# Product of du and B for both channel halves in one 1024-wide VectorE instruction, with the states in a ring of three pairs

## What is computed

```
def step(state, xs):                       # 256 steps along the tokens
    d_t, B_t, C_t, u_t = xs
    dA = jnp.exp(d_t[..., None] * A)
    state = state * dA + (d_t * u_t)[..., None] * B_t[:, None, :]
    y_t = jnp.einsum('ben,bn->be', state, C_t)
    return (state, y_t)
...
x = x + tanh(g_xattn) * ssm(ctx, layernorm(x))       # y = (scan + D*u) * silu(z)
x = x + tanh(g_ffn) * routed_moe(layernorm(x))       # 8 experts, top 2, hidden width 512
```

## Time and profile before

| | |
|---|---|
| median of 3 runs | 307.88 us (307.65 to 309.58) |
| time of the profiled execution | 307.61 us |
| its span | 305.8 us |
| PE busy | 265.8 us (87%) |
| DVE (VectorE) busy | 229.0 us (75%) |
| ACT (ScalarE) busy | 188.4 us (62%) |
| POOL (GpSimd) busy | 183.2 us (60%) |
| mean granted TensorE clock | 0.959 of full |

### The profile page before, as it was taken

One profiled execution on the slowest core, in us unless ns is written; L12 is line 12 of the kernel. 1 busy time (PEld: TensorE's weight loads), 2 busy tenths in 40 slices (PEclk: granted clock), 3 DMA queues, 4 the chain that ended last, 5 costly groups with the idle time before them and its releaser, 6 DMA issues.

```text
span 305.8 us, 4685 instructions
## 1 busy us (share of the span) xinstructions
PE 265.8 (87%) x1166; PEld 178.1 (58%) x1167; DVE 229.0 (75%) x398; ACT 188.4 (62%) x349; POOL 183.2 (60%) x162
## 2 busy tenths in 40 slices
PE   8984698789788999897889489999999999999970
PEld 8432243234234345363565357988889898888960
DVE  2839999997889999999899664656565665656640
ACT  1894577865765685768484844565665657566540
POOL 5000449996999898998590442355547465565442
PEclk9996979999999999999999778999999999999996
DMA  7699200000000000001059611123242332423222
GB/s 233 225 395 387 94 2 0 0 1 0 0 0 3 1 0 0 0 2 69 1 184 331 242 49 39 29 41 57 48 69 40 63 51 52 68 35 69 28 26 34
DMA packets 16659, 22.70 MB, mean 74 GB/s; under 512 B 2554, under 2 KB 10274, under 8 KB 16642
## 3 DMA queue, kind: packets, MB, share of 16 engines
q1 hardware_dynamic: 11456, 16.41, 15.2%
q0 software_dynamic: 4416, 6.03, 11.9%
q10 hardware_dynamic: 770, 0.06, 0.2%
HBM read 17.38 MB, written 5.11 MB: 74 GB/s over the span
## 4 chain that ended last, share of the span: by engine, by line
PE 54%; DVE 23%; issue 11%; ACT 6%; POOL 3%; POOLq 1%; DVEq 0%; ACTq 0%
PE PD L1025 11%; PE PZ L1061 11%; PE PU L1025 10%; PE PY L844 7%; DVE states L1216 6%; DVE states L1222 5%; PE PY L1047 3%; DVE u L1142 2%; POOL hC L411 2%; PE PZ L1016 2%; PE PU L823 1%; PE PU L830 1%; PE PU L752 1%; ACT PD L612 1%; DVE WO L1240 1%
## 5 line engine op out<-in xcount | busy, mean ns | idle before, releaser
L411 POOL TENSOR_TENSOR hC<-states,WO 128x512 f32<-128x512 f32 x63 | 79.5, 1272 | 19.6 <-DVE states L1222 9.2
L1222 DVE TENSOR_TENSOR_SCAN states<-PD,states 128x512 f32<-128x512 f32 x64 | 77.3, 1209 | 1.3 <-ACT PD L612 1.0
L844 PE MATMUL PY<-hC,ident 128*128 128x512 f32 x128 | 68.9, 623 | 7.2 <-POOL hC L411 6.9
L446 POOL DMA_INDIRECT out<-lg,y_at x23 | 36.4, 1581 | 49.3 <-ACT lg L718 41.9
L612 ACT ACTIVATE PD<-WO,Aneg 128x510 f32<-128x510 f32 x64 | 43.9, 688 | 18.2 <-DVE states L1222 15.5
L1216 DVE TENSOR_TENSOR states<-PU,WO 128x512 f32<-128x512 f32 x64 | 42.7, 668 | 2.7 <-POOL hC L411 1.6
L402 POOL TENSOR_TENSOR W_lo<-W,W_hi 128x512 fp32r<-128x512 f32 x25 | 32.5, 1308 | 11.5 <-ACT W_hi L523 11.5
L1459 DVE TENSOR_TENSOR dA<-PU,dA 128x512 f32<-128x512 f32 x23 | 15.9, 691 | 28.5 <-PE PU L1025 28.5
L702 ACT ACTIVATE hidT_hi<-PY 128x512 fp32r<-128x512 f32 x23 | 13.8, 598 | 38.0 <-PE PY L1047 38.0
L1471 DVE TENSOR_TENSOR WO_lo<-WO,WO_hi 128x512 fp32r<-128x512 f32 x46 | 29.7, 688 | 9.4 <-issue 9.3
L844 PEld LDWEIGHTS PY<-hC,ident 128*128 128x128 f32 x128 | 21.9, 191 | 23.4 <-POOL hC L411 17.3
(11 more groups left out here) (245 smaller groups left out, 507.2 us busy)
## 6 DMA issues: line engine op xcount, KB each, us to landing
W<-in_L_ffn_w SPq DMA_DIRECT2D x16, 512.0 KB, 10.9
WO<-in_L_ffn_wo SPq DMA_DIRECT2D x8, 512.0 KB, 8.4
xs<-in_x SPq DMA_DIRECT2D x2, 512.0 KB, 5.5
out<-xs SPq DMA_DIRECT2D x2, 512.0 KB, 3.2
x_rows<-u SPq DMA_DIRECT2D x2, 512.0 KB, 5.9
early<-in_ctx SPq DMA_DIRECT2D x1, 512.0 KB, 4.2
hC<-x_rows,x_at POOLq DMA_INDIRECT x23
out<-lg,y_at POOLq DMA_INDIRECT x23, 3.8
```

Of the source, the lines that this page charges most:

```text
L411: pool.tensor_tensor(hC[:, n % 2, :], states[:, n % RING, :], C_rep[:, pair % C_RING, :], ALU.mult).then_inc(hc_done, 1)
L446: pool.indirect_dma_start(out=out, out_offset=bass.IndirectOffsetOnAxis(ap=y_at[:, s:s + 1], axis=0), in_=y_tile[s % 2], in_offset=None, c ...
L844: pe.matmul(PY[:, h, :], ident[:, :], hC[:, n % 2, :], start=False, stop=(m == DS - 1)).then_inc(y_done, 1)
L1222: dve.tensor_tensor_scan(states[:, n % RING, :], DEC[n % 2], states[:, n % RING, :], 0.0, ALU.mult, ALU.add).then_inc(scan_done, 1)
```

## The change

The products of the two halves of a pair become one VectorE instruction of 128 x 1024: B is read twice through a stride of zero, du of both halves stands side by side already. Pair 0 keeps two narrow products (`first_drive`), since du of its second half comes later; the first counts up a semaphore of its own, `half_driven`. The slots are now in pairs: RING = 3 pairs, two of them in `states` (which stays at 4 slots, 2 * (RING - 1)), the third in `dA`. Pair p lies in slot (p + 1) % 3, slot 0 is `dA`, first used by pair 2, whose product therefore also waits for two logarithms (`sp_ln_ok`) and two roundings (`rest_ok`). The product of pair p waits for the hC product of state 2p - 5. `dbu_done` now counts pairs: 32 in all for 64, and its waits are halved.

```
-RING = 4
+RING = 3
...
-        states = sb("states", [P, RING, QT])
+        states = sb("states", [P, 2 * (RING - 1), QT])
...
+        def state_pair(pair):
+            slot = (pair + 1) % RING
+            return states[:, 2 * slot - 2:2 * slot, :] if slot else dA[:, :, :]
+        def state(n):
+            return state_pair(n // 2)[:, n % 2, :]
...
                 if pair:
-                    pe.wait_ge(dbu_done, 2 * pair)
+                    pe.wait_ge(dbu_done, pair)
...
-            def drive(n):
-                q, pair, h = n // (2 * DS), n // 2, n % 2
+            def first_drive(h):
+                dve.wait_ge(b_ps, 1)
+                dve.wait_ge(du_ok, h + 1)
+                dve.tensor_tensor(state(h), BCR[0], du[h], ALU.mult).then_inc(dbu_done if h else half_driven, 1)
+            def drive(pair):
+                q = pair // DS
                 dve.wait_ge(b_ps, pair + 1)
-                dve.wait_ge(du_pool if q else du_ok, h + 1)
-                if n >= RING:
-                    dve.wait_ge(hc_done, n - RING + 1)
-                dve.tensor_tensor(states[:, n % RING, :], BCR[pair % 2], du[2 * q + h], ALU.mult).then_inc(dbu_done, 1)
+                dve.wait_ge(du_pool if q else du_ok, 2)
+                if pair == RING - 1:
+                    dve.wait_ge(sp_ln_ok, 2)
+                    dve.wait_ge(rest_ok, 2)
+                if pair >= RING:
+                    dve.wait_ge(hc_done, 2 * (pair - RING + 1))
+                dve.tensor_tensor(state_pair(pair), BCR[pair % 2].rearrange("p (o t) -> p o t", o=1).to_broadcast((P, 2, QT)),
+                                  du_sb[:, q, :, :], ALU.mult).then_inc(dbu_done, 1)
...
             def through(at, end):
                 for n in range(at, end):
-                    if n + 1 < NT:
-                        drive(n + 1)
+                    if n % 2 and n + 1 < NT:
+                        drive(n // 2 + 1)
                     scan(n)
...
-            drive(0)
+            first_drive(0)
             scan(0)
             delta_sum(1)
             drive_input(1)
-            drive(1)
+            first_drive(1)
```

More of the change, by code:

```diff
@@ L257, in build @@
         diag_ok, gz_ok, x2_ps, logits_ok = sem("diag_ok"), sem("gz_ok"), sem("x2_ps"), sem("logits_ok")
+        half_driven = sem("half_driven")
         exp_done, dbu_done, scan_done, hc_done, y_done = map(sem, ("exp_done", "dbu_done", "scan_done", "hc_done", "y_done"))
@@ L337, in _ @@
             sp.wait_ge(exp_done, NT)
-            sp.wait_ge(dbu_done, NT)
+            sp.wait_ge(dbu_done, NT // 2)
             load_WO(0)
@@ L410, in times_C @@
                         pool.wait_ge(y_done, n - 1)
-                    pool.tensor_tensor(hC[:, n % 2, :], states[:, n % RING, :], C_rep[:, pair % C_RING, :], ALU.mult).then_inc(hc_done, 1)
+                    pool.tensor_tensor(hC[:, n % 2, :], state(n), C_rep[:, pair % C_RING, :], ALU.mult).then_inc(hc_done, 1)
                     if n in SPLIT_AT:
@@ L984, in _ @@
                 add_gz(1, r)
-            pe.wait_ge(dbu_done, NT)
+            pe.wait_ge(dbu_done, NT // 2)
             pe.wait_ge(c_ok, NT // 2)
@@ L1207, in _ @@
             rounding(1)
-            def drive(n):
-                q, pair, h = n // (2 * DS), n // 2, n % 2
-                dve.wait_ge(b_ps, pair + 1)
-                dve.wait_ge(du_pool if q else du_ok, h + 1)
-                if n >= RING:
-                    dve.wait_ge(hc_done, n - RING + 1)
-                dve.tensor_tensor(states[:, n % RING, :], BCR[pair % 2], du[2 * q + h], ALU.mult).then_inc(dbu_done, 1)
+            def first_drive(h):
[4 more added lines that the diff above has]
+                q = pair // DS
+                dve.wait_ge(b_ps, pair + 1)
+                dve.wait_ge(du_pool if q else du_ok, 2)
[6 more added lines that the diff above has]
+                                  du_sb[:, q, :, :], ALU.mult).then_inc(dbu_done, 1)
             def scan(n):
                 dve.wait_ge(exp_done, n + 1)
-                dve.wait_ge(dbu_done, n + 1)
-                dve.tensor_tensor_scan(states[:, n % RING, :], DEC[n % 2], states[:, n % RING, :], 0.0,
-                                       ALU.mult, ALU.add).then_inc(scan_done, 1)
+                if n:
+                    dve.wait_ge(dbu_done, n // 2 + 1)
+                else:
+                    dve.wait_ge(half_driven, 1)
+                dve.tensor_tensor_scan(state(n), DEC[n % 2], state(n), 0.0, ALU.mult, ALU.add).then_inc(scan_done, 1)
             def through(at, end):
                 for n in range(at, end):
-                    if n + 1 < NT:
-                        drive(n + 1)
+                    if n % 2 and n + 1 < NT:
+                        drive(n // 2 + 1)
                     scan(n)
@@ L1406, in _ @@
             dve.wait_ge(scan_done, NT)
-            dve.tensor_tensor(hC[:, 1, :], states[:, (NT - 1) % RING, :], C_rep[:, (NT // 2 - 1) % C_RING, :], ALU.mult).then_inc(last_hc, 1)
+            dve.tensor_tensor(hC[:, 1, :], state(NT - 1), C_rep[:, (NT // 2 - 1) % C_RING, :], ALU.mult).then_inc(last_hc, 1)
             best_two(0)
```

## The result

The changed kernel takes 311.0 us (median of 4 runs, 309.9 to 311.7) where the kernel before took 308.0 beside it (307.65 to 309.6): a ratio of 1.0082, 95% interval 1.0041 to 1.0122. The forecast was 306.7 with a range to 308.9. The likeliest case, "within 1%", came, on the wrong side and outside the range. In a later comparison, on another chip, the same kernel stood at 1.0029 (1.0007 to 1.0052): slower, by 0.3 to 0.8%.

A forecast was written before the change was run, and what follows sets the result against it. VectorE looked like the bound, with GpSimd near full from 76 to 100 us and VectorE tied to a GpSimd-TensorE chain. Gains 0.3 + 0.3 + 0.6 = 1.2 us took 307.61 to 306.4, median 306.7; range 303.9 to 308.9.

The forecast's parts named there:

- within 1%: Outcome class for the whole kernel: time changes by less than about 3.1 us either way; chance 0.76.
- The wide product: VectorE, scan stage: one 1024-wide product takes 1.11 us against 1.16 for two narrow ones, 0.05 saved each.
- 31 of them, no ring waits: VectorE, scan stage: 31 products become wide, 1.5 us less work; waits for the ring (1.6 + 0.8 us) go.
- Where VectorE is pinned: Places where VectorE waits on a chain through GpSimd and TensorE, so savings elsewhere are waited away; total gain 1.2 us.
- VectorE is the bound: Rival: VectorE bounds throughout, so its 1.5 us and 4.7 us of waits count fully: 6.2 us, time 301.7; chance 0.10.
- the full fixed part: Rival: each removed VectorE instruction saves its whole fixed cost; wide product 1.02 us, some 3.4 gained, time 304.5; chance 0.10.
- odd scans too late: Rival: odd scans, 0.53 us later, delay GpSimd at six waits; 2.0 us slower, 309.9; chance 0.10, with what is worse.
- (a): The ramp, up to rounding 2 on VectorE: summed lengths give 0.16 us later, taken as no gain and no loss.
- 0.3 + 0.3 for the C broadcasts: TensorE's C broadcasts wait less for VectorE's product: 0.3 us gained at 64.49 us and 0.3 at 117.55.
- (e): Behind the first logits: three narrow products become one wide, last hC product 6.3 us behind them for 6.92; 0.6 gained.
- the rest shifts as one: Routing, gathers and expert loop have the same instructions and move together, with no further gain or loss.
- the pins: Places tying VectorE to GpSimd and TensorE: ramp, step-size sums (scan 22), second gating product, second base logits up to the router.

The follow-up runs named there:

- e7: Changed kernel with the mean and last hC products kept clear of GpSimd, plus three zero-adding TensorE matmuls behind state 6's sum: 0.9917 of the kernel before.
- e4: Kernel before with the mean product moved earlier and GpSimd's first splits held until VectorE's last hC product, as a control: 1.0003 of the unedited kernel before.
- e1: Changed kernel with the small mean product moved ahead of scan 1, where GpSimd waits anyway: 1.0003 of the kernel before.
- e2: Changed kernel with GpSimd waiting for VectorE's last hC product before its first four weight splits: 1.0006 of the kernel before.
- e3: Changed kernel with the mean product moved ahead of scan 1 and GpSimd's first splits held until VectorE's last hC product: 0.9972 of the kernel before.
- e15: Changed kernel with narrow products for the first 32 states and wide ones for the last 32: 1.0073 of the kernel before.
- e6: Changed kernel with each wide product written as two narrow ones at the same place in VectorE's order: 1.0058 of the kernel before.
- e8: Changed kernel with both GpSimd collisions removed and, from pair 10 on, ScalarE's C row copy one decay earlier: 1.0014 of the kernel before.

## Why the prediction failed, step by step

- **The wide product**, 1.11 us start to start, right: 1.11 to 1.12. **31 of them, no ring waits**: right.
- **Where VectorE is pinned**, right in place: scan 22 idles 1.73 us (said: near 2), the second gating product 1.08 (over 1), the logits wait for the router 1.02. So the saving of 1.5 us in VectorE's work is waited away, as said, and neither "VectorE is the bound" nor "the full fixed part" had a case. GpSimd's waits for the scan are 10.8 us where 9.2 stood; the rival "odd scans too late" was nearest to the time (309.9) but is not what happened, since from state 34 to the logits the stretch is equal.
- **(a) "I take no gain and no loss" in the ramp: the step that failed.** The sum took every length on VectorE as fixed and asked only where VectorE's own instructions move. It did not ask what GpSimd does beside each of them. The new order put GpSimd's hC product of state 2 under a 0.16 us instruction that stands in the sum's stretch: +1.0 us on rounding 2. And the 1.26 us wait of the B row was quoted in that very step as something that follows, and not as an idle time that could grow: the new order makes it 2.36 us by itself and 2.74 with the collision, and the clock's fall behind it costs another 0.55.
- **0.3 + 0.3 for the C broadcasts**: of the sum to the logits, 0.6, e7 shows 0.28 against the kernel before (115.52 for 115.80) and nothing against e4 (115.36). Mis-sized, at most half of it there.
- **(e) behind the logits, 6.3 for 6.92**: the product came 6.54 us behind them, after 0.44 of waiting for TensorE. To its end 7.22 for 7.62 with the collision gone: 0.4 for 0.6. And 8.27 with it: "the rest shifts as one" failed on one instruction, the last hC product, whose neighbour on GpSimd had been 0.11 us behind it and was 0.09 ahead.
- **The range** held only mechanisms of waiting on semaphores. Two collisions of about 1 us, one clock drop of 0.55 and 0.25 outside the span, all of one sign, are some 2.9 us, and the forecast's gain of 1.2 shrank to about 0.7 (0.28 + 0.4). That leaves 2.2 of the 2.98 us between the profiled executions; 0.65 of the rest lie in the expert loop and behind the last matmul, and no run asked why. The medians of the later comparison differ by only 0.85 us (310.42 and 309.57), so how much of the 2.2 a typical execution pays stays open. The forecast was also made from an execution at a good clock: of the 30 runs of the kernel before beside e7 (307.7 to 310.7 us), the time falls by some 1.5 us per 0.01 of mean granted clock (correlation -0.92; clocks 0.947 to 0.964, median 0.953), and the profiled one had 0.959.

## What to carry to other kernels

When a change shifts VectorE against GpSimd, list every VectorE instruction with two SBUF inputs, however small, and the casts and tensor_scalars between SBUF buffers too, and look at what GpSimd runs beside it before and after: one that was free can cost the rest of a whole GpSimd instruction. Treat TensorE's idle stretches of 1 to 3 us as places to watch, also where TensorE only gets its earlier work done sooner: one that grew from 1.3 us to 2.4 cost a fall of the clock. Where one lies on the path, a few matmuls that change nothing can keep the clock, as they did here. And when engines pace one another, a saving on the fullest one is worth what the pins let through, here 0.7 us of 1.5.

## What the runs showed of the hardware that was not expected

- A VectorE product of four columns takes 0.15 us alone, 0.52 us in the middle of a GpSimd product and 1.09 to 1.16 us near its start; for 512 columns it is 0.70 and 1.73. GpSimd's split pays in turn when VectorE is first by 0.11 us: 1.71 for 1.27. On the seam between two GpSimd instructions it costs nothing. One SBUF input can be enough: a tensor_scalar of four columns took 1.24 us for 0.16, ending 0.03 us behind GpSimd's instruction, and a cast of 16 columns took 1.20 beside GpSimd's splits.
- TensorE's granted clock fell to the lower level behind idle times of 2.4 to 2.9 us that ended at 51.8 to 54.0 us in all six executions that had them unfilled (changed twice, e1, e2, e3, e15), and not behind 1.3 to 1.6. In e6 (2.25 us) and e8 (1.98) it did not fall there, but had been low at 34 to 42 us (0.79). Four late matmuls kept it at 1.0 from 174 to 178 us, where it was 0.5 in e3.
- The kernels with wide products have 0.25 us more between time and span, and half of the products wide was not enough to show it.
